# A fused two-layer decoder: every self-attention slot before every cross-attention slot, scores issued ahead of values, router bias added by VectorE

## The reference, cut to what matters

```
x = x + self_attention(layernorm(x))           # 16 heads, causal
x = x + cross_attention(layernorm(x), ctx)     # 16 heads, window of 8 by segment id
h = layernorm(x)
logits = h @ gate_w.T + gate_b                 # router over 32 experts
top4, idx = top_k(logits, 4)                   # then experts, and the second layer
```

## Time and profile before

| | before |
|---|---|
| median of 3 runs | 978.79 us (977.43 to 978.91) |
| the profiled execution's own time | 973.44 us |
| its span, first to last instruction | 971.7 us |
| mean granted TensorE clock | 0.887 |
| busy share of the span | PE 79%, DVE 76%, ACT 54%, POOL 53% |

### The profile page before, as it was taken

The page is one execution under the profiler, slowest core; times in us unless marked ns, Lnnn a source line. Parts: engine busy times, 40 slices in busy tenths (PEclk is TensorE's granted clock), DMA queues, the critical chain, the costliest instruction groups (busy, mean ns, idle before and its releaser), DMA issues. The chain is left out here.

```text
span 971.7 us, 14566 instructions
## 1 busy us (share of the span) xinstructions
PE 766.5 (79%) x4345; PEld 541.1 (56%) x4345; DVE 737.8 (76%) x1499; ACT 520.7 (54%) x1349; POOL 517.0 (53%) x535
## 2 busy tenths in 40 slices
PE   6798999999999998139999705785999999960265
PEld 3477888888888766037777503333555555540133
DVE  2585777777777855777777656977899999769976
ACT  0223456555555645016666403578888788309085
POOL 1003777777777864725555274303799788623210
PEclk9879999999999989569999957986999999985577
DMA  8806100000000400014545554002223232010000
GB/s 282 279 0 269 79 2 1 1 7 7 1 6 7 166 21 11 7 32 139 149 145 137 117 176 150 1 3 108 78 96 109 87 105 92 20 44 0 0 16 28
DMA packets 30047, 72.43 MB, mean 75 GB/s; under 512 B 5507, under 2 KB 19587, under 8 KB 27475
## 3 DMA queue, kind: packets, MB, share of 16 engines
q1 hardware_dynamic: 25362, 58.92, 17.4%
q0 software_dynamic: 4608, 12.59, 5.4%
HBM read 60.94 MB, written 10.55 MB: 74 GB/s over the span
## 5 line engine op out<-in xcount | busy, mean ns | idle before, releaser
L1735 POOL TENSOR_TENSOR arena<-arena 128x1024 f32<-128x1024 f32 x63 | 147.4, 2372 | 31.2 <-DVE arena L1701 31.2
L1701 DVE TENSOR_TENSOR_SCAN arena<-arena,ps 128x1024 f32<-128x1024 f32 x64 | 143.5, 2276 | 13.9 <-PE ps L1622 8.5
L1642 PE MATMUL ps<-arena 128*128 128x512 f32 x256 | 120.1, 593 | 0.0
L776 ACT ACTIVATE arena<-arena 128x128 f32<-128x128 f32 x256 | 98.8, 390 | 12.2 <-DVE arena L723 12.1
L608 PE MATMUL ps<-arena 128*128 128x128 f32 (+1 forms) x768 | 98.2, 279 | 0.8 <-PEq L345 0.8
L1032 POOL DMA_INDIRECT arena<-tokens,arena x64 | 61.7, 964 | 66.6 <-PE ps L1053 48.9
L819 POOL TENSOR_TENSOR arena<-arena 128x256 f32<-128x256 f32 x64 | 47.6, 744 | 89.6 <-DVE arena L709 89.6
L608 PEld LDWEIGHTS ps<-arena 128*128 128x128 f32 (+1 forms) x768 | 92.4, 195 | 1.4 <-issue 1.2
L784 ACT ACTIVATE arena<-ps 128x512 f32<-128x512 f32 x64 | 38.2, 597 | 96.8 <-PE ps L627 96.8
L718 DVE TENSOR_TENSOR arena<-ps,arena 128x512 f32<-128x512 f32 x64 | 44.1, 689 | 55.5 <-PE ps L618 55.5
L1667 ACT ACTIVATE arena<-arena 128x1016 f32<-128x1016 f32 x64 | 72.6, 1135 | 23.1 <-DVE arena L1701 23.0
(11 more groups left out here) (321 smaller groups left out, 1667.3 us busy)
## 6 DMA issues: line engine op xcount, KB each, us to landing
arena<-c_rows SPq DMA_DIRECT2D x32, 512.0 KB, 3.6
arena<-in_E_gu SPq DMA_DIRECT2D x8, 1024.0 KB, 12.1
expert_out<-arena SPq DMA_DIRECT2D x64, 128.0 KB, 2.3
arena<-in_E_dn SPq DMA_DIRECT2D x1, 4096.0 KB, 12.9
arena<-in_ctxT SPq DMA_DIRECT2D x2, 1024.0 KB, 4.9
arena<-in_X_o SPq DMA_DIRECT2D x1, 2048.0 KB, 20.5
arena<-in_A_o SPq DMA_DIRECT2D x1, 2048.0 KB, 27.5
arena<-in_F_w SPq DMA_DIRECT2D x2, 1024.0 KB, 5.4
```

What stands on the lines that cost most here:

```text
L776: t = eng.activation(pr[:, i % 3, j, :], sm[:, d, j, :], ACT.Exp, bias=negm[:, d, j:j + 1], scale=SCALE[slots[i][0]], accum_out=rsum[:, i ...
L1642: t = eng.matmul(ps[:, 2 * k + half, :], ident, hC[s % 4][:, half * 512:(half + 1) * 512], start=False, stop=n == ST - 1)
L1701: eng.tensor_tensor_scan(hst[s % 4], dA[s % 4], psD[s % 2].rearrange("p k m -> p (k m)"), 0.0, ALU.mult, ALU.add).then_inc(h_ready, 1)
L1735: eng.tensor_tensor(hC[s % 4], hst[s % 4], Csb[i % 4], ALU.mult).then_inc(hC_ready, 1)
```

## The change

`ALONE` becomes 32, so that `order` has all A slots and then all X slots. In each turn TensorE issues scores ahead of values. The router's bias is no longer added by a one-row matmul: it is loaded into all 128 partitions, and VectorE adds it while it reads the logits from PSUM, in place of ScalarE's copy.

```diff
-                load(eng, "gate", gate_b[0:1, :], a["E_gate_b"])
+                load(eng, "gate", gate_b, a["E_gate_b"])
...
-        ALONE = 12
+        ALONE = NB * NG
...
                         for c in range(DC):
-                            eng.matmul(ps[:, 4, 0:E], hT[:, c, b * P:(b + 1) * P], gate_w[:, c, :], start=c == 0, stop=False)
-                        t = eng.matmul(ps[:, 4, 0:E], ones[0:1, :], gate_b[0:1, :], start=False, stop=True)
+                            t = eng.matmul(ps[:, 4, 0:E], hT[:, c, b * P:(b + 1) * P], gate_w[:, c, :],
+                                           start=c == 0, stop=c == DC - 1)
...
                         output(t - 6)
+                    if 0 <= t - 2 < SLOTS_A:
+                        scores(t - 2)
                     if 0 <= t - 5 < SLOTS_A:
                         values(t - 5)
-                    if 0 <= t - 2 < SLOTS_A:
-                        scores(t - 2)
...
+                def logits(b):
+                    eng.wait_ge(small_done, end_no["X", b] + 1)
+                    eng.tensor_tensor(logit[:, b], ps[:, 4, 0:E], gate_b, ALU.add).then_inc(small_ready, 1)
...
                         normed(*turn_at[t])
+                    if t in after_at and after_at[t][0] == "X":
+                        logits(after_at[t][1])
                     if t - 1 in after_at and after_at[t - 1][0] == "X":
                         best(after_at[t - 1][1])
...
                         name, b = after_at[t]
-                        eng.wait_ge(small_done, end_no[name, b] + 1)
                         if name == "A":
+                            eng.wait_ge(small_done, end_no[name, b] + 1)
                             eng.activation(LX["qc"][0:QC, b * P:(b + 1) * P], ps[0:QC, 4, 0:P], ACT.Copy).then_inc(small_ready, 1)
-                        else:
-                            eng.activation(logit[:, b], ps[:, 4, 0:E], ACT.Copy).then_inc(small_ready, 1)
```

More of the change, by code:

```diff
@@ L2159 @@
     put("E_gate", chunked(g["L0_ffn_gate_w"].T))
-    put("E_gate_b", g["L0_ffn_gate_b"].reshape(1, E))
+    put("E_gate_b", np.tile(g["L0_ffn_gate_b"].reshape(1, E), (P, 1)))
     put("E_bias", np.stack([g["L0_ffn_b_gate"].T, g["L0_ffn_b_up"].T], -1))
```

## The result

The changed kernel takes 989.73 us (median of 4 runs, 988.61 to 991.09) against 978.5 for before in the same comparison: a ratio of 1.0117, 95% interval 1.0100 to 1.0135, so 10 to 13 us slower. The forecast was 988.3, +9.5.

What follows compares the result with a forecast made beforehand. TensorE's issue was taken to bound most turns, the residual wait adjacent X batches. Boundaries +14.2, bias -2.15, drain -0.95 and -0.6, last boundary -1.0 sum to +9.5: 988.3 us on the median, own range 984 to 991; 979.5 to 993.5 with rivals.

Steps and rivals of the forecast that it cites:

- router turns, five: Router turns of five X batches: no bias matmul (0.33) and queries' first load hidden (0.1), 0.43 us each, -2.15.
- the stretch with the last boundary: Last boundary, where TensorE idled 1.76 us: earlier mask add, no bias, no rope in the way; 1.0 won, bounds 0.5 and 1.76.
- the drain: End of the block: TensorE no longer idles for mixed behind the bias, -0.95 us; very last bias off the path, -0.6.
- Turns: TensorE's steady turns: scores ahead of values only moves the tile-width switch, so turns stay 4.76 (A) or 3.87 us (X).
- Rival 1: Values' weight load: the reorder wins TensorE's own 0.09 us a turn, -5.4 over about 60 turns, 982.9; chance 0.14.
- rival 2: Values' weight load: the wait for ScalarE is real, all 0.33 us a turn goes, -19.8, total 968.5; chance 0.08.
- The boundaries: Between adjacent X batches output waits for the residual: 1.83 us first, five at 2.55 plus 1.61 clock; +14.2 against before.
- the start of rope: VectorE's rope starts 0.20 us behind turn_probs in plain turns; logits ahead of softmax makes that 0.92 at later boundaries.
- none for the first: Clock behind the first boundary's 1.67 us idle: no fall, so no 1.61 us, unlike the five with 2.4 idle.
- The hidden parts: Wider bias load, down weights sent 19 slots sooner, SyncE's h stores and GpSimd's rotate: covered, so no time added.
- Rival 4: Boundaries: VectorE gains nothing, six keep their price or more at 4.2 to 4.8 us; +13 to +17, about 994; chance 0.10.
- Rival 3: The clock doesn't fall at the boundaries: -8.0 us, leaving +1.5, 980.3, within 0.2%; chance 0.08.

Runs made afterwards that it cites:

- LAG 7: The changed kernel with LAG of the X batches 7 instead of 8, so the residual moves one turn ahead of the waiting output: 965.59 us, ratio 0.9908 to before.
- the filler: The changed kernel with seven more 128x128 fp32 matmuls, unused by the result, ahead of each of the seven waiting outputs: 981.27 us, ratio 1.0032 to before.
- logits moved: The changed kernel with logits behind softmax of its turn on VectorE, instead of ahead of it: 979.25 us, ratio 1.0018 to before.

## Why the prediction was right

**The sum.** +9.5 was forecast, the block measured +10.0 and the timed ratio +11.4 (10 to 13). That the total came so near is partly luck: the boundaries cost 3.0 more than forecast, and 2.5 came back in terms that were forecast at nothing or too small.

| term | forecast | measured |
|---|---|---|
| each of five boundaries over a plain turn | 4.16 | 4.37 |
| first boundary | 1.83 | 3.72 |
| all, against 8.4 of before | +14.2 | +17.2 |
| router turns, five | -2.15 | -2.2 |
| the stretch with the last boundary | -1.0 | -1.2 |
| the drain | -1.55 | -2.2 |
| scores first, in the fill and at norms | 0 | -1.6 |

The measured figures are differences of the metronome: (8.22 + 8.26 + 8.24 + 8.25 + 8.25) / 5 - 3.87 = 4.37; 7.59 - 3.87 = 3.72; 5 x (4.76 - 4.31); the last five turns 17.21 instead of 18.39; from the last copy to the end of the block 8.24 instead of 10.47. The last row is what the rows above it leave of the metronome's total, 298.24 - 286.01 = +12.23. It is near what the first 37 turns show, which are 171.11 us against 172.96 with the order alone.

**Turns: right.** 4.76 and 3.87 in all profiles with scores first. The time lost at a change of tile width accounts for it and moved with values: output to scores takes 0.87, scores to values 0.99, and the copy that values needs had ended at 119.67 + 0.60 = 120.27, 1.06 us before values starts at 121.33. Rival 1 and rival 2 are out.

**The boundaries: right in mechanism, two terms too small.** The residual is what they wait for (LAG 7 removes all of it), the clock's 1.61 is 1.60 (the filler), and logits ahead of softmax is what makes VectorE late (logits moved). The step that was mis-sized is the start of rope. I had it 0.20 and 0.92 behind turn_probs; it came at 0.56 and 1.17. In both places softmax's last instruction, line 723, took 0.58 and 0.71 us instead of 0.17. The step that failed is the clock's "none for the first": its idle was 1.99 instead of 1.67, and the clock fell, 1.6 us. These two make the difference of 3.0; gains at the edges that I had at zero took 1.6 back and the drain 0.7.

The failed step rests on a premise that the runs refute, that the length of the idle decides. The trace of before already had a case against it: the first of its own boundaries idled 1.81 and was followed by the lower level.

```profile
340.60:341.60 1.00, 1.00 (x5) 0.28 (x4) 0.00 (x0) 0.00 (x0) 0.92 (x3) 0.50 0.46 146
```

Over all profiles idles of 1.66, 1.67, 1.76, 1.99 (logits moved), 2.58 (the order alone) and 2.61 (the changed kernel in the old order, shown here) left the clock up; others of 1.67, 1.81, 1.83, 1.99 and 2.43 to 2.61 were followed by a fall. So the late rope by itself doesn't explain why the clock fell at the first boundary, and the cause stays open.

```profile
354.81 1.10 PE L646 MATMUL ps<-arena 128*128 128x256 f32 x4 [2.61 <-DVE arena L734]
```

```profile
354.80:356.80 2.00, 2.00 (x14) 1.78 (x16) 0.50 (x2) 0.00 (x0) 1.84 (x4) 1.00 0.00 0
```

**The hidden parts: right.** The down weights' load is sent 19 slots sooner and lands in 13.4 us instead of 12.9; the turns around it are 3.87 and 4.04 like the rest. The wider bias left no mark.

**Rival 4, that VectorE gains nothing, was nearer than I gave it.** The boundary went from 4.20 to 4.37 in spite of scores that come 0.67 sooner. Scores first shortened the wait when alone (idle 1.83 for 2.43, the boundary 7.52 for 8.07); logits undid that (2.61 at the same place with both edits in the old order). **Rival 3** had its point in that the clock need not fall: in that same place, behind 2.61 idle, it didn't.

**The single edits against the whole.** By the profiles they sum to 16.9 - 5.2 - 6.0 = +5.7, or +7.3 without the 1.6 in the fill that the bias edit can't have caused, and together they make +10.0. The boundaries account for most of what is left: with the other two edits they cost 25.6 above plain turns instead of 25.2 in the new order, and 5.3 instead of 8.2 in the old one. Some of that is which boundaries had a fall of the clock in the one execution profiled, and the timed ratios sum to +1.45% against +1.17% together, so that the parts hinder each other is not shown.

**What stays open.** Why the clock fell behind some idles and not behind others of the same length, and so how many falls another execution would have; and how much of the bias edit's gain is real: the profile says 4, its timing 1 with 2 either way.

## What to carry to other kernels

When an order of work is changed, count how often each wait between groups occurs in either order, and price one occurrence from the trace; here the steady turns were equal and the loss was in six waits that had been two. An instruction that waits should stand behind the ready ones on its engine: one line on VectorE, moved behind softmax, took 0.9 us out of each of five waits. A regular order can permit a shorter lag that a mixed one forbids, so see whether the new order makes an old margin unnecessary.

## What the hardware showed that I had not expected

**A tiny VectorE instruction ends with GpSimd's.** Line 723 multiplies 128x4 numbers by a constant, SBUF to SBUF. It has a minimum of 0.169 us, in the kernel before a median of 0.170, in the changed one a median of 0.417 and a maximum of 0.724. With scores first (alone or in the whole change) the timing shifted so that it often starts inside one of GpSimd's two 64x256 adds of rotate, mostly line 829: 40 times of 64 with over 0.17 us of the add left, against 12 times before and 12 with the order alone. Each of those 40 took 0.30 us or more and ended 0.02 to 0.04 us after the add. Two that keep their length:

```profile
255.57 0.72 POOL L829 TENSOR_TENSOR arena<-arena 64x256 f32<-64x256 f32 x1
...
256.20 0.17 DVE L723 TENSOR_SCALAR arena<-arena 128x4 f32<-128x4 f32 x1
...
259.68 0.17 DVE L723 TENSOR_SCALAR arena<-arena 128x4 f32<-128x4 f32 x1
259.80 0.72 POOL L829 TENSOR_TENSOR arena<-arena 64x256 f32<-64x256 f32 x1
```

These don't meet it long enough: GpSimd's add ends 0.09 behind the start of one and begins behind the start of the other. An instruction of one column on GpSimd did not have this effect: in the trace of before three of line 723 started with 0.45 us of line 837 left, 128x1, and took 0.17. At the boundary above GpSimd's runs from 292.04 to 292.76 and line 723 from 292.07 to 292.78. The Trainium skill ("SBUF — State Buffer", "SBUF: two separate sides") states that VectorE, in a two-port mode, and GpSimd take a shared pair of ports as an exclusive lock for a whole instruction. By that rule the four columns wait until the whole other instruction is done; the trace agrees for the 64x256 adds, not for line 837, and whether line 723 runs in a two-port mode no trace shows. No run took the overlap away, so the cause is read from these times and not tested. Rope starts right behind line 723 at both boundaries, so its 0.4 to 0.5 us delay rope, the residual and output.

**The fall of the clock mostly has one price here.** It is 1.61, 1.60 and 1.61 us in three ways (output, values and scores against their full-clock lengths; with and without filler; two like boundaries with logits moved). With the order alone one fall lasted longer, and that boundary took 9.45 where the one without a fall took 6.69 and the other four 7.95 to 8.14. Keeping TensorE at work during the wait avoided it six times out of six; a shorter idle did not do so reliably.
